# Causal attention on one core: batch-chunk-group order, alternating row halves, short pieces of weighted values, mask on VectorE

## The reference, cut to what matters

```python
# x: (2, 1024, 128) fp32, 16 heads of 8 columns
x = x + layernorm(attention(layernorm(x), w_qkv, w_out, head_scales, head_dirs))
x = x + layernorm(moe(layernorm(x), router_w, ...))     # top 2 of 7 experts, and a shared one
# attention:
scores = einsum('bhqd,bhkd->bhqk', q, k) / sqrt(8)
scores = where(tril(ones(T, T)), scores, -inf)
scores = scores + head_scales * q_proj[..., :, None] * k_proj[..., None, :]   # rank 1: folded into wq
out = einsum('bhqk,bhkd->bhqd', softmax(scores), v)
```

## Time and profile before

| | us |
|---|---|
| median of 3 runs (505.12 to 507.33) | 506.38 |
| the profiled execution | 507.76 |
| its span, first to last instruction | 506.0 |
| PE busy (as modelled), share of the span | 88% |
| DVE busy | 64% |
| ACT busy | 51% |
| POOL busy | 26% |

### The profile page before, as it was taken

How to read it: one execution, slowest core, us unless ns; L and a number is a source line. 1 busy time by engine, 2 the same in 40 slices (tenths; PEclk the granted TensorE clock), 3 DMA queues, 4 the chain that set the end, 5 groups by cost and what they waited for, 6 DMA issues and landing times. The chain is left out here.

```text
span 506.0 us, 10925 instructions
## 1 busy us (share of the span) xinstructions
PE 445.1 (88%) x4076; PEld 277.6 (55%) x4076; DVE 321.5 (64%) x860; ACT 256.0 (51%) x450; POOL 133.8 (26%) x222
## 2 busy tenths in 40 slices
PE   1745998999999999999999968898899999999970
PEld 0523252534435353443534436455599999999970
DVE  3975978888787888888784682749723333333233
ACT  1430146676666767677677743845224343444313
POOL 9400000000100000000100001534367676764303
PEclk9985559999989999999989985989999999999986
DMA  3065374100202010000000006210077787777242
GB/s 109 1 170 162 87 196 138 52 15 2 66 1 66 4 56 10 2 2 4 3 3 1 2 2 171 78 43 0 17 249 237 238 236 230 243 236 228 72 166 84
DMA packets 39031, 46.59 MB, mean 92 GB/s; under 512 B 5635, under 2 KB 26500, under 8 KB 38980
## 3 DMA queue, kind: packets, MB, share of 16 engines
q1 hardware_dynamic: 36548, 40.91, 27.1%
q0 software_dynamic: 2432, 4.99, 3.4%
HBM read 34.80 MB, written 10.88 MB: 90 GB/s over the span
## 5 line engine op out<-in xcount | busy, mean ns | idle before, releaser
L613 ACT ACTIVATE probs<-banks 128x1024 f32<-128x1024 f32 (+1 forms) x192 | 146.2, 813 | 63.1 <-PE banks L472 43.3
L748 DVE TENSOR_REDUCE mx_part<-banks 128x1 f32<-128x512 f32 (+3 forms) x256 | 132.6, 582 | 22.9 <-PE banks L448 15.0
L448 PE MATMUL banks<-k_st,q_st 48*128 48x512 bf16 (+3 forms) x384 | 122.7, 360 | 14.9 <-DMA k_st<-k_rows 11.9
L465 PE MATMUL banks<-q_st,k_st 51*128 51x512 bf16 (+3 forms) x384 | 100.6, 337 | 3.3 <-ACT probs L613 1.9
L484 PE MATMUL banks<-probs,v_pad 128*32 128x512 f32 (+3 forms) x768 | 84.3, 512 | 0.1
L1514 DVE TENSOR_TENSOR hidden<-banks,gate 128x512 f32<-128x512 f32 x38 | 26.3, 692 | 66.4 <-PE banks L1152 64.9
L465 PEld LDWEIGHTS banks<-q_st,k_st 51*128 51x128 bf16 x384 | 32.2, 95 | 54.7 <-ACT probs L613 43.0
L748 DVE TENSOR_REDUCE mx<-banks 128x1 f32<-128x512 f32 (+3 forms) x128 | 53.8, 481 | 13.0 <-PE banks L454 12.7
L448 PEld LDWEIGHTS banks<-k_st,q_st 48*128 48x128 bf16 x384 | 34.6, 95 | 46.4 <-DVE mx_part L748 28.0
L452 PE MATMUL banks<-mask_qk,ident_half 64*128 64x128 bf16 x256 | 57.0, 233 | 0.0
L470 PE MATMUL banks<-mask_kq,ident_half 64*128 64x128 bf16 x256 | 50.5, 221 | 0.0
(11 more groups left out here) (204 smaller groups left out, 608.4 us busy)
## 6 DMA issues: line engine op xcount, KB each, us to landing
w_g<-in_w_gate SPq DMA_DIRECT2D x38, 256.0 KB, 3.2
w_u<-in_w_up SPq DMA_DIRECT2D x38, 256.0 KB, 4.3
q_rows<-parts SPq DMA_DIRECT2D x24, 128.0 KB, 2.4
k_rows<-parts SPq DMA_DIRECT2D x24, 128.0 KB, 2.4
q_st<-q_rows SPq DMA_DIRECT2D x32, 96.0 KB, 2.3
k_st<-k_rows SPq DMA_DIRECT2D x32, 96.0 KB, 2.3
w_d<-in_w_down SPq DMA_DIRECT2D x8, 256.0 KB, 4.9
back<-results SPq DMA_DIRECT2D x4, 512.0 KB, 5.7
```

The costliest lines, as they stand in the source:

```text
L448: last = nc.tensor.matmul(dst[:, 0:width], q_st[r][rows, c, p, (i % CH) * P:(i % CH + 1) * P], k_st[r][rows, kc, p, 0:width], start=True, ...
L465: last = nc.tensor.matmul(dst[a][:, 0:width], k_st[r][rows, j // CH, p, (j % CH) * P:(j % CH + 1) * P], q_st[r][rows, c, p, first:BANK], s ...
L613: nc.scalar.activation(probs[unit % PROBS][:, 2 * p:2 * p + 2, first:BANK], slot_pair[k % 2].rearrange("p (a t) -> p a t", a=2)[:, :, 0:BA ...
L748: nc.vector.tensor_reduce(dst, max_bank[m % RING][:, 0:width], AX.X, ALU.max, negate=True).then_inc(max_taken, 1)
```

## The change

The diff, cut to what acts on the work. `STEPS` is a list of (score unit, maxima unit); a unit of `SCORES` and of `MAXIMA` is now (item, u), an item a (batch, chunk, group).

```diff
-ONES_BITS = float(np.array([0x3F803F80], np.uint32).view(np.float32)[0])
+MINUS_ONES_BITS = float(np.array([0xBF80BF80], np.uint32).view(np.float32)[0])
-PROBS = 3
+PROBS = 4
+ITEMS = ([(0, c, g) for c in range(NC) for g in range(NG)]
+         + [(1, c, g) for c in reversed(range(NC)) for g in range(NG)])
+AHEAD_FIRST, AHEAD_LATER = 2 * CH, 3 * CH
+def step_list():
+    steps = [(None, m) for m in range(AHEAD_FIRST)]
+    for s in range(len(SCORES)):
+        if s == NG * CH:
+            steps += [(None, s + m) for m in range(AHEAD_FIRST, AHEAD_LATER)]
+        m = s + (AHEAD_FIRST if s < NG * CH else AHEAD_LATER)
+        steps.append((s, m if m < len(MAXIMA) else None))
+    return steps
+HEADS = ((0, 1), (0, 0), (1, 1), (1, 0))
+PIECES_AT = {-1: 2, 0: 2, 1: 2, 2: 1, 3: 1}     # pieces of 128 columns after each pair
+        while ready <= s - 2:                    # value_plan(): values lag by two units
+            left += cuts(ready)
+def rows_with(s, p):       # the turned maxima of the next item ride in the slot of own unit 1
+def outputs_with(s, p):    # the turned outputs of the last item in the slots of own unit 2
```

In the queues and on the engines (L numbers are of the kernel before):

```diff
 SP
-            load_stacks(0, 0)
-            store_parts(0, 1)
-            load_stacks(0, 1)
-            load_stacks(1, 0)
-            load_stacks(1, 1)
-            send_rows(0, 0)
+            for r in range(NG):
+                load_stacks(0, r, 0)
+            for r in range(NG):
+                send_rows(r)
+                load_stacks(0, r, 1)
             for half in range(2):
                 store_parts(1, half)
+                send_rows(NG + half)
 POOL
-                nc.gpsimd.memset(v_pad[:, n, :, :, :], 0.0)          # x8, and x8 of the ones
-                nc.gpsimd.affine_select(out=ident_half / mask_qk / mask_kq ...)      # x12
+            nc.gpsimd.memset(v_ones[:, :, :, :, HD:HD + 1], 1.0)
+            nc.gpsimd.affine_select(out=mask_max[:, BANK - P:], ...)                  # x1
+            def select(s, p):      # own units: zero the 128 x 128 above the diagonal, 2 heads
+                pool.wait_ge(slot_taken, SLOT_AT["score", s, p] + 1)
+                nc.gpsimd.affine_select(out=own, in_=own, compare_op=ALU.is_ge, fill=0.0, base=0,
+                                        pattern=[[0, 2], [1, P]], channel_multiplier=-1)
 PE
-                if diagonal is not None: (two mask matmuls in maxima, two in score)
+            for s, m in STEPS:
+                if s is not None and SCORES[s][1] == 0 and m is not None:
+                    three maxima, score(s, 0, 0), score(s, 0, 1), weighted_values(VALUES[s, 0]),
+                    maxima(m, HG - 1), score(s, 1, 0), score(s, 1, 1), weighted_values(VALUES[s, 1])
+                else:
+                    for p in range(PAIRS_G):
+                        for a in range(2):
+                            if m is not None:
+                                maxima(m, 2 * p + a)
+                            if s is not None:
+                                score(s, p, a)
+                        if s is not None:
+                            weighted_values(VALUES[s, p])
+                if s == item_end(NG * NC + NG) + 1:
+                    first_turn_attn()
+                if s == item_end(NG * NC + NG) + 3:
+                    first_project()
 weighted_values
-                    last = nc.tensor.matmul(o_bank[h * HQ:(h + 1) * HQ, first:BANK], v_pad[...],
-                                            probs[unit % PROBS][:, h, first:BANK], ...)
+                    last = nc.tensor.matmul(o_bank[h * HQ:h * HQ + HD + 1, at:end], v_ones[...],
+                                            probs[s % PROBS][:, h, at:end], ...)
+                    # neighbouring pieces of a unit go as one matmul per head
 ACT
+            act.wait_ge(parts_ready, 2)     # 12 DMAs: the parts of batch 0, chunk 1
+            for qk, dst in ((0, q_rows), (1, k_rows)): ... act.dma_start(...)
 DVE (take_maxima)
-                        nc.vector.tensor_reduce(dst, max_bank[m % RING][:, 0:width], AX.X, ALU.max,
-                                                negate=True)
+                    if kc == c:
+                        nc.vector.tensor_tensor_reduce(masked[e % RING][:, 0:width], src,
+                                                       mask_max[:, BANK - width:], 1.0, NEG,
+                                                       ALU.add, ALU.max, accum_out=dst)
+                    else:
+                        nc.vector.tensor_reduce(dst, src, AX.X, ALU.max)
```

More of the change, by code:

```diff
@@ new lines, in item_end @@
+def item_end(k):
+    return sum(BLOCKS[c] for _, c, _ in ITEMS[:k + 1])
+def rows_with(s, p):
+    k = SCORES[s][0] + 1
+    return k if own_unit(s) == 1 and p == 0 and k < len(ITEMS) and k not in TURNED_ALONE else None
+def outputs_with(s, p):
+    k = SCORES[s][0] - 1
+    return k if own_unit(s) == 2 and k >= 0 else None
+VALUES, VALUES_LEFT = value_plan()
+SUMS_AFTER = {}
+for at, done in VALUES.items():
+    for s, first in done:
+        if first == BANK - P and s + 1 == item_end(SCORES[s][0]):
+            SUMS_AFTER[at] = SCORES[s][0]
@@ L110, in slot_list @@
+def slot_list():
+    slots = []
+    for s, m in STEPS:
+        if s is not None:
+            slots += [("score", s, p) for p in range(PAIRS_G)]
+        slots += [("rows", k) for k, at in TURNED_ALONE.items() if at == m]
+    slots.append(("out", len(ITEMS) - 1))
     return slots
 SLOT_AT = {what: k for k, what in enumerate(slot_list())}
+for s in range(len(SCORES)):
+    for p in range(PAIRS_G):
+        if rows_with(s, p) is not None:
+            SLOT_AT["rows", rows_with(s, p)] = SLOT_AT["score", s, p]
+        if outputs_with(s, p) is not None:
+            SLOT_AT["out", outputs_with(s, p)] = SLOT_AT["score", s, p]
@@ new lines, in _ @@
+            for s, m in STEPS:
+                if s is not None:
+                    k, u = SCORES[s]
+                    if u == 0 and 2 <= k < len(ITEMS) - 2:
+                        normalise(k - 2)
+                    if own_unit(s) >= 0:
+                        for p in range(PAIRS_G):
+                            select(s, p)
+                if m is not None and m + 1 == item_end(done):
+                    split_rows(done)
+                    done += 1
+            for k in range(len(ITEMS) - 4, len(ITEMS)):
+                normalise(k)
@@ new lines, in _ @@
+            for s, m in STEPS:
+                if s is not None:
+                    for p in range(PAIRS_G):
+                        exponentials(s, p)
+                        if (s, p) in SUMS_AFTER:
+                            take_sums(SUMS_AFTER[s, p])
+                for k, at in TURNED_ALONE.items():
+                    if at == m:
+                        act.wait_ge(slot_filled, SLOT_AT["rows", k] + 1)
+                        take_rows(k, slot_bank[SLOT_AT["rows", k] % 2][0][:, 0:P]).then_inc(slot_taken, 1)
@@ new lines, in invert_sums @@
+            def invert_sums(k):
+                dve.wait_ge(slot_taken, SLOT_AT["out", k] + 1)
+                nc.vector.reciprocal(inverse[k % 4][:, :], o_raw[k % 4][:, :, HD]).then_inc(sums_inverted, 1)
+            dve.wait_ge(consts_ready, 1 + 3)
+            inverted = 0
+            for s, m in STEPS:
+                if m is not None:
+                    take_maxima(m)
+                    if s is not None and own_unit(s) == 3 and SCORES[s][0] > 0:
+                        invert_sums(SCORES[s][0] - 1)
+                        inverted += 1
```

499 lines of the change are left out of this document (231 added, 268 removed).

## The result

The changed kernel takes 480.69 us, the median of four runs (477.46 to 482.73); the kernel before took 506.86 us beside it (505.12 to 507.66, the three runs of above and a fourth). The ratio is 0.9483, with a 95% interval of 0.9445 to 0.9520: some 26 us less, where 12 had been forecast. The direction was right. Ratios leave out executions more than 1.5% above their kernel's fastest (one or two each in e1, e5, e9, e12 and e13), medians don't, and e9's trace is of such an execution, 499.94 us.

The account below looks back on a forecast made before the run. DVE's maxima were taken as the nearest floor, with some 4.8 us per group lost to PE. Step prices summed to M = 260.3, 12.1 us saved, so a median of 494.3, rounded to 495 us (range 483 to 516).

Parts of the forecast that it names:

- the stage of maxima alone: Start of attention: eight units of maxima before any scores, 16.2 us on DVE, ending at 55.2.
- there by then: Claim that item 0's turned rows would have arrived before the first scores, so no wait.
- d: Extra DVE cost of each add-and-max over a reduce in own units, taken as 0.08 us.
- M: Time at which DVE's maxima end, 272.4 us before the change, forecast at 260.3.
- rival B: Mask is free, d = 0, and PE sets own steps: 10 us less, 485 us; chance 0.15.
- price of a step = the largest of DVE, PE and ACT in it: Pricing rule for each attention step; gave 8.5 us per four own units, 9.84 per four full.
- The two dips in mid-attention: Two falls of the clock to 1.2 GHz in mid-attention, priced at 1.2 us each.
- The first steps with scores at 1.2 GHz: Early score steps at the low clock, PE 4.4 us against DVE's 2.8; 2.0 us added.
- The second stage alone: Four units of maxima without scores after item 3: 8.1 us, plus 1.0 for warming up again.
- Behind M no gain: Work after the last maximum: remaining steps, projection, norms and router were to take as long as before.
- Rival C: PE gives it back: passages between products and values 0.1 us dearer, or clock falls more often; 501 us, chance 0.14.
- DVE hardly waits: Claim about full units of the kernel before: twelve maxima of three units in one row of 7.37 us.

Follow-up runs that it names:

- e1: Changed kernel with a plain reduce in place of each of the 256 add-and-max on DVE, causal mask left out of the maxima: 479.48 us, ratio 0.9454.
- e5: Changed kernel with the values of a step in one block behind the second pair, instead of one behind each pair: 488.20 us, ratio 0.9624.
- e9: Changed kernel with a 128x128 fp32 memset on DVE ahead of each add-and-max: 489.02 us, ratio 0.9665.
- e12: e8 plus unread PE products: 36 of 512 columns during the wait for the first stacks, one behind each lone product of maxima: 489.39 us, ratio 0.9673.
- e13: e8 plus one unread PE product of 128 columns behind each product of maxima that stands alone: 487.74 us, ratio 0.9607.
- e11: Changed kernel with one block of values per step and own slots for turned maxima and outputs: 490.48 us, ratio 0.9705.
- e2: Changed kernel with a one-column memset on DVE ahead of each of the 256 add-and-max: 478.56 us, ratio 0.9454.
- e3: Kernel before without its mask matmuls in maxima and scores, causal mask left out altogether: 497.83 us, ratio 0.9845.
- e14: Kernel before with batch 0's second stores issued by ACT and without its mask matmuls: 495.06 us, ratio 0.9776.
- e10: Kernel before with the stores of batch 0's second half of the parts issued by ACT instead of SP: 501.15 us, ratio 0.9918.
- e4: Changed kernel with mask matmuls back on PE, plain reduces and no selects on POOL: 488.37 us, ratio 0.9653.
- e7: Changed kernel with each product of maxima on the same row half as the score behind it: 486.98 us, ratio 0.9613.
- e8: Changed kernel with maxima twelve units ahead of the scores from the start, instead of eight for chunk 0 and twelve later: 475.95 us, ratio 0.9396.

## Why the prediction was wrong in size

**The start was right, in part by luck.** First maximum on DVE 38.93 (39.0), first exponential 55.33 (55.2): the earlier trace rows has 68.14. But the stage of maxima alone ended at 52.96, 2.2 us before its forecast, and then the first scores waited 1.34 us for item 0's rows (54.69), which the prediction had "there by then". The two misses cancel at the first exponential. The sum of the changed kernel held the gain of the stacks' loads, since it was built from the front, but the prediction didn't know it: the 5.48 us of waiting in the kernel before were never named.

**The term that failed first is d, "I take 0.08, near the batched spacing".** It measures 0.01 or less, and I count it as nothing here. In the sum it stands 32 times before the first scores (2.6 us), 16 in the second stage alone (1.3), and 0.5 in each of 13 blocks (6.5): 10.4 us of the 14.1 by which M was missed. This was rival B's mechanism, to which 0.15 was given. The evidence lay in the trace of the kernel before: a single reduce of 512 columns is recorded with 0.69 us, and twelve take 7.37, 0.61 each, so each lies beside the next for 0.08 us. I took the spacing of small instructions among small ones instead.

**The second is "price of a step = the largest of DVE, PE and ACT in it".** With the mask free it gave 8.0 us for an own block and 8.1 with the reciprocal; 7.65 is measured with the merge. Added up over the block, the forecast's terms are 2.2 + 2.2 + 2.15 + 1.2 = 7.75 for PE and 6.8 for DVE, and the larger sum is near what was measured; the largest of each step is not. I read it so: the three banks carry work over, PE fills them ahead in the 512-column step, where DVE is the slower, and DVE lives on them in the next. No run changed the number of banks, so that reading is argued from the rows. It is 0.45 us in 13 blocks, 5.9 us, and one reason why rival B's 485 was too high.

**The clock's terms partly cancel.** The two dips in mid-attention, 2.4 us, didn't come in this execution. The first steps with scores at 1.2 GHz were taken at 2.0 us. By the merge of item 4 the kernel stood at 90.65 instead of 92.9; d alone should have brought it to 88.8 and the block sums to 87.5, so the low clock, with DVE's idle 0.87 us at the first scores' wait for their rows, cost 3 us more than I gave it. The second stage alone cost another 2.5 beyond its 1.0 us. Full blocks at 9.75 instead of 9.84 gave 0.8. In sum: -10.4 - 5.9 - 2.4 - 0.8 + 3 + 2.5 = -14.0, against 246.2 - 260.3 = -14.1. The forecast for the profiled execution, 495.7, was 18.2 us too high; the other 4 us lie behind M.

**"Behind M no gain" was off by 2.8 us**: 31.6 instead of 34.4 us, and 1.4 less after the block. The cause stays open: with one block and own slots in the new order (e11) it was 33.0, but 32.8 also in e2, which has the changed kernel's pieces and slots.

**What the prediction said of PE held by term and failed by use.** Rival C didn't come: own blocks have PE busy for 7.37 of 7.55 us, yet they are shorter than forecast. The passages between products and values are paid (1.09 us from one block of values to the next in a full half step, 172.06 to 173.15), and they are paid where PE had time.

Against my reading, the mask's products had been only some 1.1 of the 4.8 us per group that DVE lost. A group of the old order is two own blocks and a full one: 28.67 us before, 27.5 without masks (e3, e14), 2 x 8.49 + 10.07 = 27.05 in e11, 2 x 7.65 + 9.75 = 25.05 in the changed kernel. So of 3.6 us the mask has 1.1, the order 0.5, pieces and slots 2.0. And not all was lost to PE. These rows of the kernel before lie in one group, from the end of its first own block into its full units, where the prediction has "DVE hardly waits":

```profile
193.29 0.26 DVE L733 RECIPROCAL inverse<-o_raw 128x16 f32<-128x16 f32 x1 [1.16 <-ACT o_raw L633]
...
202.58 2.48 DVE L748 TENSOR_REDUCE mx_part<-banks 128x1 f32<-128x512 f32 x4 [0.21 <-PE banks L448]
205.66 0.25 DVE L733 RECIPROCAL inverse<-o_raw 128x16 f32<-128x16 f32 x1 [0.59 <-ACT o_raw L633]
```

Of the 4.6 us of waiting in this group, 1.75 stand in front of the two reciprocals, for ACT's copy of the turned outputs (the first still in the own units). In the changed kernel and in e11 these waits are gone, in e3 and e14 they are still there. No run takes them away alone, so what they cost by themselves isn't known.

**POOL hid its selects**: 0.41 us each for 256 elements, half of what I allowed, 52.4 us in all; 5.8 us of PE's weight loads waited for them, PE itself 0.5.

Where the 5.2% come from, in the order in which the runs peel them off: the loads 0.8 (e10), the mask 1.4 (e14 against e10), the order by chunk 0.7 (e11 against e14), pieces and slots 2.2 (the changed kernel against e11), of which the pieces are 1.4 (e5). Each share is known to some 0.5, so the order's isn't clear of noise. They depend on the order of peeling: the mask is worth 1.7 in the new order (e4). Alternating halves is in both kernels and has no share; without it e7 loses 1.3.

## What to carry to other kernels

Price an added instruction on a pipelined engine by whether it fits into the overlap of its neighbours, and not by how fast small ones follow each other. Where a ring of buffers stands between two engines, add up each engine's work over as many steps as the ring can bridge, and then ask separately for the one longest thing that blocks the filling engine: it must be shorter than what the ring holds. And before pricing what a change adds, list the longest waits of the bound engine in the kernel before, one by one; the largest single one here, 5.48 us in the start stage, was in no term.

## What the runs showed of the hardware

- An accumulator's read on DVE takes 0.08 us in the record and 0.01 or less in the spacing of the operations around it (changed kernel against e1); between operations of 512 columns a memset of one column adds 0.01 (e2), one of 128 columns 0.08 (e9).
- The add-and-max of PSUM and an SBUF mask has nearly the plain reduce's rate: 0.61, 0.48, 0.35 and 0.21 us of spacing for 512, 384, 256 and 128 columns, with two blocks of all four widths at 14.03 us against 13.69 (e1).
- POOL's select in place takes 0.41 us for 128x256 fp32, the same as for 128x128.
- PE's clock stayed at 1.2 GHz for some 68 us, from 42 to 110, while PE was busy nearly all the time (e13). It came back at 69 us in the changed kernel, 79 in e8, 87 in e12, 94 in e7; without the mask's products, with less for PE to do, it came back later (about 86 us in e3 and 81 in e14) than with them (about 75 in the kernel before and 72 in e10). Each is one execution. No rule that these runs show fits them all. The Trainium skill (TensorE: Matmul & The Clock Gate, Part 1: The HAM clock gate) lets the clock follow how busy PE has been; these rows don't agree, and the measurement stands.
